# Typed edge pass of a graph network kernel: sums by node from a bf16 one-hot matrix and three bf16 parts, finished in the next block's turn

## What is computed

```python
W = jnp.einsum('rb,bio->rio', comp, basis)
msg = node_feats[src] * norm
seg = etype.astype(jnp.int32) * N + dst
s = jax.ops.segment_sum(msg, seg, num_segments=R * N)
s = s.reshape(R, N, -1)
h = jnp.einsum('rni,rio->no', s, W) + bias
```

## Time and profile before

| What | Value |
|---|---|
| Median of three runs | 11435.95 us |
| Profiled execution, its own time | 11445.84 us |
| Its span, from first to last instruction | 11442.9 us |
| Mean granted TensorE clock | 0.767 of full speed |
| Busy in the span: PE, DVE, ACT, POOL | 61%, 60%, 24%, 56% |
| Typed pass, about | 564 to 4637 us |

### The profile page before, as it was taken

How to read it: one execution, slowest core, us unless ns; L and a number is a source line. 1 busy time by engine, 2 the same in 40 slices (tenths; PEclk the granted TensorE clock), 3 DMA queues, 4 the chain that set the end, 5 groups by cost and what they waited for, 6 DMA issues and landing times. The chain is left out here.

```text
span 11442.9 us, 147532 instructions
## 1 busy us (share of the span) xinstructions
PE 6980.6 (61%) x54285; PEld 5438.7 (48%) x54333; DVE 6860.1 (60%) x8420; ACT 2795.3 (24%) x2578; POOL 6424.7 (56%) x6751
## 2 busy tenths in 40 slices
PE   9955555555555555699999999443434333333435
PEld 4433333333333333599989999332323233333324
DVE  5488888888888888422232222566666656565665
ACT  4333333333333333300000000222221212121212
POOL 4377777777777777100000000577777777777775
PEclk9966767767666766899999999766666666666667
DMA  9933333333333333599979998444444444444443
GB/s 385 392 123 129 127 129 127 132 125 134 123 134 123 134 124 132 180 355 355 356 270 356 356 356 317 122 113 107 113 108 112 110 110 111 109 112 108 113 107 75
DMA packets 588593, 2032.55 MB, mean 178 GB/s; under 512 B 195913, under 2 KB 354051, under 8 KB 463235
## 3 DMA queue, kind: packets, MB, share of 16 engines
q1 hardware_dynamic: 310210, 1292.34, 33.5%
q0 software_dynamic: 207360, 318.92, 12.2%
q10 hardware_dynamic: 70944, 420.31, 10.1%
HBM read 1396.53 MB, written 634.49 MB: 177 GB/s over the span
## 5 line engine op out<-in xcount | busy, mean ns | idle before, releaser
L1252 POOL DMA_INDIRECT big<-Pd,mt x3240 | 3062.2, 945 | 1077.3 <-issue 987.2
L402 POOL DMA_INDIRECT big<-Yd,ix x3240 | 3062.2, 945 | 1017.8 <-issue 987.2
L496 PE MATMUL ps<-ring 128*128 128x490 bf16 x3240 | 1420.7, 538 | 1711.5 <-DVE ring L438 1711.5
L1363 PE MATMUL ps<-big 128*128 128x384 bf16 x2160 | 567.7, 425 | 2497.2 <-DVE big L1286 2497.2
L435 DVE TENSOR_TENSOR ring<-ps,vw 128x2940 bf16<-128x2940 f32 x540 | 1736.3, 3215 | 480.2 <-PE ps L498 479.9
L496 PEld LDWEIGHTS ps<-ring 128*128 128x128 bf16 x3240 | 418.5, 129 | 2475.5 <-issue 1629.9
L1363 PEld LDWEIGHTS ps<-big 128*128 128x128 bf16 x2160 | 246.3, 120 | 2720.0 <-DVE big L1286 2528.9
L629 PE MATMUL ps<-big,cb 128*128 128x192 bf16 x13230 | 1115.2, 246 | 0.0
L629 PEld LDWEIGHTS ps<-big,cb 128*128 128x128 bf16 x13230 | 1084.7, 98 | 11.4
L516 ACT ACTIVATE Z<-ps 128x1470 bf16<-128x1470 f32 x544 | 778.3, 1467 | 1254.1 <-PE ps L498 1254.1
L516 ACT ACTIVATE big<-ps 128x1470 bf16<-128x1470 f32 x536 | 766.5, 1468 | 1267.4 <-PE ps L498 1267.4
(11 more groups left out here) (218 smaller groups left out, 11670.8 us busy)
## 6 DMA issues: line engine op xcount, KB each, us to landing
Yd<-big SPq DMA_DIRECT2D x196, 1024.0 KB, 8.8
Aj<-Z SPq DMA_DIRECT2D x68, 2940.0 KB, 9.5
big<-Aj SPq DMA_DIRECT2D x136, 1470.0 KB, 8.4
cb<-Aj ACTq DMA_DIRECT2D x136, 1470.0 KB, 8.5
Aj<-big SPq DMA_DIRECT2D x67, 2940.0 KB, 9.5
cb<-Aj SPq DMA_DIRECT2D x134, 1470.0 KB, 8.4
Z<-Aj ACTq DMA_DIRECT2D x134, 1470.0 KB, 8.4
dr<-in_dstr SPq DMA_DIRECT2D x137, 1152.0 KB, 7.7
```

Of the source, the lines that this page charges most:

```text
L402: e.indirect_dma_start(gv[j][:, k, 0:64], None, table, bass.IndirectOffsetOnAxis(ap=ix[j][:, k:k + 1], axis=0)).then_inc(sm[f"g{j}"], 16)
L496: nc.tensor.matmul(PS[q][:, 0:W * NT], olo[r][:, c, :], one[r][:, c, :], start=True, stop=False)
L1252: e.indirect_dma_start(gv[j][:, k, :], None, Pd, bass.IndirectOffsetOnAxis(ap=mt[j][:, k:k + 1], axis=0)).then_inc(sm[f"g{j}"], 16)
L1363: last = nc.tensor.matmul(ag, oh[j][:, k, :], parts[q][:, 3 * P * c:3 * P * (c + 1)], start=(k == 0), stop=(k == K - 1))
```

## The change

The rows are no longer summed in float32. Each weighted row is split into three bf16 parts, `part[:, 0]` the rounded row, `part[:, 1]` the rounded rest and `part[:, 2]` the rounded rest of that; a column of ones, with zeros in parts 1 and 2, still counts the edges. ScalarE makes the first two parts (`high`, `middle`), VectorE the two differences (`middle`, `low`). `oh` is now bf16 and serves as the weights; the 195 columns of the parts are the moving matrix. The result lies with the nodes on the partitions, so VectorE adds the three parts up (`add_parts`), TensorE transposes the sum (`turn_sums`), and `add` takes it from there. All of it for block b-1 stands in block b's turn. POOL waits for `lo`, the end of `low`, where it waited for `pe`.

```diff
-            gv = [big[:, K * 65 * j:K * 65 * (j + 1)].rearrange("p (k f) -> p k f", f=65) for j in range(2)]
-            o0, o1 = K * 130, K * 130 + K * P
-            oh = big[:, o0:o1].rearrange("p (k n) -> p k n", n=P)
+            gv = [big[:, K * 64 * j:K * 64 * (j + 1)].rearrange("p (k f) -> p k f", f=64) for j in range(2)]
...
+            oh = big[:, o0:o2].bitcast(BF16).rearrange("p (k n) -> p k n", n=P)
+            part = big[:, o2:o1].bitcast(BF16)[:, 0:K * PW].rearrange("p (k s f) -> p s k f", s=3, f=65)
...
 def gpsimd
-                        e.wait_ge(sm["pe"], reg(e, b))
+                        e.wait_ge(sm["lo"], reg(e, b))
...
 def vector
+                def middle(j, n):
+                    e.wait_ge(sm["hi"], n)
+                    nc.vector.tensor_tensor(gv[j], gv[j], part[:, 0, :, 0:64], ALU.subtract).then_inc(sm["rs"], 1)
+
+                def low(j, n):
+                    e.wait_ge(sm["md"], n)
+                    nc.vector.tensor_tensor(part[:, 2, :, 0:64], gv[j], part[:, 1, :, 0:64], ALU.subtract).then_inc(sm["lo"], 1)
+
+                def add_parts(n):
+                    e.wait_ge(sm["pe"], n)
+                    nc.vector.tensor_reduce(total[:, :], ag.rearrange("p (s f) -> p f s", s=3), AX.X,
+                                            ALU.add).then_inc(sm["sm"], 1)
...
                     group(j, 0, n)
-                    if last:
-                        e.wait_ge(sm["mul"], b)
+                    if not first:
+                        middle(1 - j, b)
                     prep(b + 1, 1 - j, 16 * (i + 1 + j), reg(e, b + 2))
+                    weight(1 - j)
                     e.wait_ge(sm["cm0"], c1)
                     group(j, 1, n)
-                    e.wait_ge(sm["pe"], n)
-                    nc.vector.tensor_tensor(oh, bc_t(iof[:, 0:P], K, P), bc_f(rl[j][:, :], K, P), ALU.is_equal)
+                    if not first:
+                        low(1 - j, b)
                     e.wait_ge(sm["cm2"], c1)
                     group(j, 2, n)
-                    if last:
-                        add(b - 1, 1 - j)
-                    weight(1 - j)
+                    if not first:
+                        add_parts(b)
+                    nc.vector.tensor_tensor(oh, bc_t(iof[:, 0:P], K, P), bc_f(rl[j][:, :], K, P), ALU.is_equal)
                     e.wait_ge(sm["cm0"], c2)
                     group(j, 3, n)
+                    if not first:
+                        add(b - 1, b)
...
 def tensor
-                    e.wait_ge(sm["mul"], n)
-                    for k in range(K):
-                        last = nc.tensor.matmul(ag[j], gv[j][:, k, :], oh[:, k, :], start=(k == 0), stop=(k == K - 1))
-                    last.then_inc(sm["pe"], 1)
+                        if before and k == 2 * GC - 1:
+                            agg(n)
+                        if before and k == 3 * GC - 1:
+                            turn_sums(b)
...
 def scalar
+                def high(j, n):
+                    e.wait_ge(sm["mul"], n)
+                    nc.scalar.activation(part[:, 0, :, 0:64], gv[j], ACT.Copy).then_inc(sm["hi"], 1)
+
+                def middle(j, n):
+                    e.wait_ge(sm["rs"], n)
+                    nc.scalar.activation(part[:, 1, :, 0:64], gv[j], ACT.Copy).then_inc(sm["md"], 1)
...
+                        high(1 - j, b)
                     e.wait_ge(sm[f"o{j}"], 16 * i + 16)
                     for t in range(TR):
...
+                        if before and t == 1:
+                            middle(1 - j, b)
```

More of the change, by code:

```diff
@@ L358, in typed_pass @@
             vw = [loc(f"vw{j}", [P, 2 * K]) for j in range(2)]
-            ag = [PS[0][0:65, P * j:P * (j + 1)] for j in range(2)]
-            pw = [PS[0][:, 2 * P + K * j:2 * P + K * (j + 1)] for j in range(2)]
+            total = loc("sums", [P, 65])
+            ag, turned = PS[0][:, 0:PW], PS[0][0:65, 2 * P:3 * P]
+            pw = [PS[0][:, 3 * P + K * j:3 * P + K * (j + 1)] for j in range(2)]
             iof = PS[1][:, 0:W * NT]
@@ L402, in turn @@
                         e.indirect_dma_start(
[L403 removed]
+                            gv[j][:, k, :], None, table,
                             bass.IndirectOffsetOnAxis(ap=ix[j][:, k:k + 1], axis=0)).then_inc(sm[f"g{j}"], 16)
@@ L413, in vector @@
                 nc.vector.memset(olo[1][:, GC - 1, :], 0.0).then_inc(sm["io"], 1)
-                for j in range(2):
-                    nc.vector.memset(gv[j][:, :, 64:65], 1.0).then_inc(sm["io"], 1)
+                for q in range(3):
+                    nc.vector.memset(part[:, q, :, 64:65], 0.0 if q else 1.0).then_inc(sm["io"], 1)
                 def prep(b, j, loaded, n):
@@ L449, in turn @@
                 def turn(b, j, i):
-                    last, b = type(b) is not int, reg(e, b)
+                    first, b = type(b) is int, reg(e, b)
                     n, c0, c1, c2 = reg(e, b + 1), reg(e, 2 * b), reg(e, 2 * b + 1), reg(e, 2 * b + 2)
-                    if last:
+                    if not first:
                         e.wait_ge(sm["cm2"], c0)
@@ L455, in turn @@
                     group(j, 0, n)
-                    if last:
-                        e.wait_ge(sm["mul"], b)
+                    if not first:
+                        middle(1 - j, b)
                     prep(b + 1, 1 - j, 16 * (i + 1 + j), reg(e, b + 2))
+                    weight(1 - j)
                     e.wait_ge(sm["cm0"], c1)
                     group(j, 1, n)
-                    e.wait_ge(sm["pe"], n)
-                    nc.vector.tensor_tensor(oh, bc_t(iof[:, 0:P], K, P), bc_f(rl[j][:, :], K, P), ALU.is_equal)
+                    if not first:
+                        low(1 - j, b)
                     e.wait_ge(sm["cm2"], c1)
                     group(j, 2, n)
-                    if last:
-                        add(b - 1, 1 - j)
-                    weight(1 - j)
+                    if not first:
+                        add_parts(b)
+                    nc.vector.tensor_tensor(oh, bc_t(iof[:, 0:P], K, P), bc_f(rl[j][:, :], K, P), ALU.is_equal)
                     e.wait_ge(sm["cm0"], c2)
                     group(j, 3, n)
+                    if not first:
+                        add(b - 1, b)
                     e.wait_ge(sm[f"g{j}"], 16 * K * i + 16 * K)
-                    nc.vector.tensor_tensor(gv[j][:, :, 0:64], gv[j][:, :, 0:64], bc_f(pw[j], K, 64),
-                                            ALU.mult).then_inc(sm["mul"], 1)
-                e.wait_ge(sm["io"], 8)
+                    nc.vector.tensor_tensor(gv[j], gv[j], bc_f(pw[j], K, 64), ALU.mult).then_inc(sm["mul"], 1)
+                e.sem_inc(sm["lo"], 1)
+                e.wait_ge(sm["io"], 9)
                 prep(0, 0, 16, 1)
@@ L477, in vector, with agg, turn_sums @@
                 blocks(e, turn)
-                e.wait_ge(sm["pe"], NB + 1)
-                add(NB - 1, 0)
+                middle(0, NB)
+                low(0, NB)
+                add_parts(NB)
+                add(NB - 1, NB)
             def tensor(e):
-                e.sem_inc(sm["pe"], 1)
+                def agg(n):
+                    e.wait_ge(sm["lo"], n)
+                    for k in range(K):
+                        last = nc.tensor.matmul(ag, oh[:, k, :], flat[:, PW * k:PW * (k + 1)], start=(k == 0), stop=(k == K - 1))
+                    last.then_inc(sm["pe"], 1)
+                def turn_sums(n):
+                    e.wait_ge(sm["sm"], n)
+                    nc.tensor.transpose(turned, total[:, :], idt[:, :]).then_inc(sm["tr"], 1)
                 def turn(b, j, i):
@@ L509, in scalar @@
                 e.sem_inc(sm["o1"], 16)
+                def high(j, n):
[4 more added lines that the diff above has]
+                    nc.scalar.activation(part[:, 1, :, 0:64], gv[j], ACT.Copy).then_inc(sm["md"], 1)
                 def turn(b, j, i):
                     done = [reg(e, 2 * b + h) for h in (1, 2)]
+                    before = type(b) is not int
+                    if before:
+                        b = reg(e, b)
+                        high(1 - j, b)
                     e.wait_ge(sm[f"o{j}"], 16 * i + 16)
@@ L516, in turn @@
                         nc.scalar.activation(aw[j][:, t], trip[t % 2], ACT.Copy).then_inc(sm[f"av{t % 4}"], 1)
+                        if before and t == 1:
+                            middle(1 - j, b)
                 blocks(e, turn)
+                high(0, NB)
+                middle(0, NB)
             choose(sm, block, {"sync": sync, "gpsimd": gpsimd, "vector": vector, "tensor": tensor, "scalar": scalar},
```

14 lines of the change are left out of this document (11 added, 3 removed).

## The result

The changed kernel takes 11627.61 us in the median of four runs (11625.70 to 11636.62), the kernel before 11434.71 us in four. The ratio is 1.017, with a 95% interval of 1.0154 to 1.0187: 193 us more. The forecast was 11629. The two profiled executions differ by less, 11627.7 to 11442.9, since the one before ran 10 us over its median; the typed pass, to the end of its last `add`, is 192.0 us longer (4828.90 against 4636.91).

The account below looks back on a forecast made before the run. POOL's gathers, 30.0 us a block, were taken to bound the typed pass. 189 us of held-off gathers plus 4 us at its end, on the median 11435.95, gave 11629 us; the 8-in-10 range was 11545 to 11720.

Parts of the forecast that it names:

- POOL bounds the pass: Typed pass: POOL's gathers, 1.250 us each, 30.0 us a block, never wait, so savings on PE are worth nothing.
- Part 1: DVE's turn in a typed-pass block: 28.8 us, between 28.3 and 30.3, so hidden under POOL's 30.0 us.
- the new wait of the reduction: DVE, after its second group and `low`, waits for PE's sums by node: 0 to 1.9 us a block, taken as 0.5.
- Part 2: `middle` and `low`, both inputs in SBUF, hold off POOL's gathers 1.61 us: 0.41 + 1.00 us a block, 189 us.
- rival C: `middle` starts just ahead of a gather, each block losing 1.61 us in place of 0.41: 11790 us; chance 0.10, half for mixtures.
- Part 3: Chain behind the typed pass's last gather: 14 to 15 us in place of 10.1, adding 4 us once.
- A: Rival: POOL is not held off by `middle` and `low`; only the pass's end costs time: 11440 us; chance 0.12.
- B: Rival: the 0.30 us of issue between gathers absorbs part of the wait, 0.81 us a block: 11549 us; chance 0.08.
- D: Rival: DVE becomes the bound, 30.3 us a turn with waits for PE and no hold: 11480 us; chance 0.03.

Follow-up runs that it names:

- e1b_both_psum: Changed kernel with the second input of `middle` and `low` from PSUM (wrong values), on a fast chip: 11441.71 us beside 11437.08 for the kernel before.
- e3b_middle_holds: Changed kernel with only `low`'s second input from PSUM, `middle` keeping two inputs in SBUF, on a slow chip: 14520.57 us beside 14201.76 for the kernel before.
- e5_halves: Changed kernel with `middle` and `low` each cut into two instructions of 768 elements, values unchanged: 11545.38 us beside 11436.96 for the kernel before.
- e1_both_psum: Changed kernel with the second input of `middle` and `low` from PSUM (wrong values), on a slow chip: 14989.47 us beside 14496.58 for the kernel before.

## Why the prediction was right

- **POOL bounds the pass; the change can only lose.** Shown. POOL waits for nothing before and after, and with the holds away the time is that of the kernel before, though 3.4 us of waits for PE are gone from DVE's turn.
- **Part 1, DVE's turn of 28.8 us.** 28.7 in e1b_both_psum. Two small errors in it nearly cancel, which is luck. One term was off: the new wait of the reduction, taken as 0.5 us with 1.9 at most, is 0.6 us in total in 111 blocks. The rest of the turn is some 0.4 us longer than its 28.3, 0.15 of it a wait for PE ahead of the third group. The 24 matmuls of 195 columns were priced at 5.2 us at most from rows of 384 columns; they end well before DVE comes. ACT's copies are 1.5 us each as taken.
- **Part 2, the hold.** Its length was taken from one copy of the last stage, 1.61 us; it is 1.62. `low` was to cost 1.00 and costs 0.96 in the mean, 129 us in 134 blocks; it starts 7.22 us behind `middle`, not 7.25. `middle` was to cost 0.41, as it does in the rows above, but costs 0.49 in the mean, 65 us: its start drifts, and in five blocks it wins just ahead of a gather and costs 1.58. That is rival C in 5 of 134 blocks, which the prediction had as a chance (0.10, mixtures included) and not as a share of its sum. Together 194 us, against the forecast's 189. All other gathers are 1.5 ns shorter than in the trace before (the group's busy time is 3057.4 us in e1b_both_psum, 3062.2 before), 5 us in the pass, and that is why the page shows 189 more. That the sum came out within 2 us is luck; within 10 it is the mechanism.
- **Part 3, the end of the pass.** Forecast 14 to 15 us for the chain in place of 10.1. The timeline of DVE after shows 4828.90 - 4814.98 = 13.9:

```profile
4814.98 1.75 DVE L494 TENSOR_TENSOR big<-big,ps 128x1536 f32<-128x1536 f32 x1 [10.78 <-DMA big<-Yd,ix]
4818.31 1.76 DVE L455 TENSOR_TENSOR big<-big 128x1536 f32<-128x1536 f32 x1 [1.57 <-ACT big L548]
4821.64 1.76 DVE L459 TENSOR_TENSOR big<-big 128x1536 bf16<-128x1536 f32 x1 [1.57 <-ACT big L552]
4827.59 0.36 DVE L463 TENSOR_REDUCE sums<-ps 128x65 f32<-128x195 f32 x1 [4.19 <-PE ps L510]
4828.62 0.28 DVE L451 TENSOR_TENSOR acc<-acc,ps 65x128 f32 x1 [0.67 <-PE ps L515]
```

- **Rivals.** A (no hold) and B (part of it absorbed in the 0.30 us between gathers) are refuted: the idle time between gathers is the same 0.30 us behind a long one (at 2526.00 and 2533.20). A spoke of a gather that reads 24 numbers of a partition; each reads one (`ix[j][:, k:k + 1]`), and even that is held off for the whole 1.62 us. C is real at the edge, in five blocks. D is refuted.
- **What the prediction did not see** is that its sum is one of a chip on which POOL sets the pace. On the two others POOL stands still in every block, and the loss is larger and of another kind.

No run with all its gathers beats the kernel before. As POOL's 3240 x 1.25 us are the pass on a fast chip, none is to be expected to that leaves the gathers as they are.

## What to carry to other kernels

Ask first which engine never waits. Here it was GpSimd (POOL), 30.0 us a block, and with 3.4 of the 3.5 us a block of VectorE's waits for TensorE gone, and the holds away, the time was still 11441.71 us beside 11437.08. Then look at every new VectorE instruction for where its inputs lie. With both in SBUF, one of 1536 elements and 1.75 us held POOL off for 1.62 us from its own start; with one input in PSUM, as the kernel before has it all along, and two such instructions a block, every gather but the pass's first took 0.94 to 0.98 us. Where that can't be had, such an instruction cost its hold less what was left until the next gather's start. A half of 768 elements with a hold of 0.82 us cost nothing when it started with a gather (at 2539.50) and 0.78 us when it started 0.04 us ahead of one (at 2507.68). Costs of several didn't add up, since each moved the gathers for the next: `low` cost 0.96 us a block behind `middle`'s hold and 1.41 without it, both in the mean.

## What the runs showed of the hardware

- The hold of `middle` or `low`, with two inputs in SBUF, was the same from its start wherever in a gather it started (e3b_middle_holds has all places): 1.61 to 1.66 us for 1536 elements, 1.62 to 1.63 in the median of a run, and 0.82 for 768 (e5_halves). POOL's side is short: a gather that started first, or up to 0.03 us later by the record (once 0.04, in e3b_middle_holds at 2619.46), delayed such an instruction by up to 0.07 us (1.82 in place of 1.75 at 1107.37). In the changed kernel the instruction won in all five blocks in which it was 0.04 or 0.05 us ahead.
- A float32 copy from SBUF to SBUF (0.95 us for 1536 elements) also stretched a gather that was already running, to 1.07 us behind the copy's start: by 0.17 to 0.32 us in nearly all blocks, and by 0.63 at most. `middle` and `low` didn't: the gather in which they started took 0.94 to 0.96 us.
- Chips differed by more than any edit of this kind: the same kernel before took 11.4 ms on some and 14.2 to 14.5 on two. POOL's issues are 1.25 us apart on all of them where nothing holds them, and the packets of a block's last gather are over 4.9 us after its issue in the median of e1_both_psum, on a slow chip (7.5 at most, but for the last block), and 2.1 us on the others. What came late there is the release of ScalarE and VectorE behind matmuls (ACT's waits on "remote" are 1433 us in 1000 to 4500 us of e1_both_psum), by a cause that is open.
